# Region attention on one core: chosen regions as four index words instead of one packed word, and a row's values stored by two DMAs instead of four

## The reference, cut to what matters

```python
q_r = pool(q).transpose(0, 2, 3, 1).reshape(N, 49, C)
k_r = pool(k).reshape(N, C, 49)
_, idx_r = jax.lax.top_k(q_r @ k_r, 4)
key_g = jnp.take_along_axis(ks_[:, :, None], idx, axis=3)
val_g = jnp.take_along_axis(vs[:, :, None], idx, axis=3)
attn = jax.nn.softmax(einsum('bhnqd,bhnkd->bhnqk', qs * SCALE, key_g), -1)
out = einsum('bhnqk,bhnkd->bhnqd', attn, val_g)
out = out + depthwise_conv3x3(v) + lepe_b
x + (einsum('nchw,oc->nohw', out, out_w) + out_b)
```

## Time and profile before

| | |
|---|---|
| median of 3 runs | 2189.56 us (2187.88 to 2190.34) |
| the profiled execution, its own time | 2192.58 us |
| its span, first to last instruction | 2190.8 us |
| busy PE, DVE, ACT, POOL | 84%, 76%, 74%, 28% |
| granted TensorE clock, mean | 0.973 |
| DMA engines, share of their time in SP's queue | 33.0% |

### The profile page before, as it was taken

One profiled execution on the slowest core, in us unless ns is written; L12 is line 12 of the kernel. 1 busy time (PEld: TensorE's weight loads), 2 busy tenths in 40 slices (PEclk: granted clock), 3 DMA queues, 4 the chain that ended last, 5 costly groups with the idle time before them and its releaser, 6 DMA issues.

```text
span 2190.8 us, 80869 instructions
## 1 busy us (share of the span) xinstructions
PE 1837.4 (84%) x25672; PEld 1200.2 (55%) x25672; DVE 1661.0 (76%) x3843; ACT 1623.5 (74%) x5017; POOL 617.6 (28%) x1920
## 2 busy tenths in 40 slices
PE   5778888898888888898888998888888988867776
PEld 3345555565555555565556655555555555545444
DVE  4678878788887878788887888878887877766544
ACT  2448878687887787788787878777887877766664
POOL 0013323232332232333232323322323232323222
PEclk9999999999999999999999999999999999998998
DMA  3213333333333333333333333333333333322323
GB/s 108 60 58 89 99 107 99 101 99 111 101 109 95 110 99 107 101 104 101 107 100 105 97 111 101 107 94 109 99 101 92 88 92 92 95 84 83 90 81 86
DMA packets 221330, 212.07 MB, mean 97 GB/s; under 512 B 19328, under 2 KB 220656, under 8 KB 220912
## 3 DMA queue, kind: packets, MB, share of 16 engines
q1 hardware_dynamic: 220912, 206.90, 33.0%
HBM read 155.45 MB, written 51.38 MB: 94 GB/s over the span
## 4 chain that ended last, share of the span: by engine, by line
SPq 69%; issue 15%; PE 8%; DMA 4%; DVE 2%; ACT 1%; POOLq 0%; POOL 0%; DVEq 0%
SPq L242 51%; SPq L210 10%; PE chunk_bank L766 4%; SPq L232 4%; DMA v_sel<-v_dram 2%; DMA v_dram<-v_stage 1%; SPq L254 1%; DVE lepe L522 1%; PE pt_bank L843 1%; SPq L259 1%; PE o_bank L857 1%; PE chunk_bank L779 1%; PE chunk_bank L755 1%; SPq L223 1%; DMA x_in<-x_dram 1%
## 5 line engine op out<-in xcount | busy, mean ns | idle before, releaser
L433 ACT ACTIVATE probs<-s_bank,neg_max 128x256 f32<-128x256 f32 x1568 | 733.6, 476 | 200.4 <-DVE neg_max L626 196.3
L313 POOL COPY k_sel<-k_all 128x128 f32 x1568 | 427.0, 307 | 1048.7 <-PE s_bank L832 1038.4
L626 DVE TENSOR_REDUCE neg_max<-s_bank 128x2 f32<-128x512 f32 x784 | 506.3, 686 | 206.7 <-PE s_bank L832 205.2
L522 DVE SCALAR_TENSOR_TENSOR lepe<-v_band,taps,lepe 128x448 f32<-128x448 f32 x896 | 612.6, 700 | 23.0 <-POOL v_band L329 13.7
L440 ACT COPY probs_t<-pt_bank 128x512 f32<-128x512 f32 x784 | 464.4, 592 | 196.7 <-PE pt_bank L843 193.5
L766 PE MATMUL chunk_bank<-xn,wqkv 128*128 128x448 f32 x1344 | 594.8, 552 | 15.0 <-ACT q_all L416 5.1
L843 PE MATMUL pt_bank<-ident,probs 128*128 128x128 f32 x3136 | 500.8, 283 | 14.3 <-ACT probs_t L440 13.0
L857 PE MATMUL o_bank<-probs_t,v_sel 128*32 128x64 f32 x12544 | 263.9, 226 | 256.9 <-DMA v_sel<-v_dram 256.0
L843 PEld LDWEIGHTS pt_bank<-ident,probs 128*128 128x128 f32 x3136 | 366.7, 143 | 157.3 <-issue 98.1
L857 PEld LDWEIGHTS o_bank<-probs_t,v_sel 128*32 128x32 f32 x12544 | 199.0, 112 | 430.8 <-DMA v_sel<-v_dram 403.1
L433 ACT ACTIVATION_READ_ACCUMULATOR probs<-s_bank,neg_max 128x1 f32 x1568 | 318.9, 203 | 0.0
(11 more groups left out here) (56 smaller groups left out, 1254.2 us busy)
## 6 DMA issues: line engine op xcount, KB each, us to landing
v_sel<-v_dram SPq DMA_DIRECT2D x1568, 64.0 KB
x_in<-x_dram SPq DMA_DIRECT2D x56, 448.0 KB, 3.9
v_dram<-v_stage SPq DMA_DIRECT2D x224, 112.0 KB
resid<-x_dram SPq DMA_DIRECT2D x56, 448.0 KB, 4.0
out_dram<-resid SPq DMA_DIRECT2D x56, 448.0 KB, 3.3
wqkv<-w_qkv_dram SPq DMA_DIRECT2D x1, 768.0 KB, 5.4
wout<-w_out_dram SPq DMA_DIRECT2D x1, 256.0 KB, 6.2
idx_row<-packed_idx SPq DMA_DIRECT2D x8, 0.2 KB
```

The costliest lines, as they stand in the source:

```text
L313: last = pool.tensor_copy(k_sel[:, r % K_SLOTS, :, RT * j:RT * (j + 1)], k_all[:, b % 2, :, bass.ds(reg[j] * RT, RT)])
L433: act.activation(probs[:, u, :], s_bank[:, u, 0:KEYS], ACT.Exp, bias=neg_max[:, r % 2, u:u + 1], accum_out=denom[:, r % 2, u:u + 1]).then_ ...
L522: ins = dve.scalar_tensor_tensor(row, v_band[:, n % BANDS, k, t // 3:t // 3 + RS, t % 3:t % 3 + W], taps[:, k, t:t + 1], row, ALU.mult, AL ...
L626: dve.tensor_reduce(neg_max[:, r % 2, 2 * hf:2 * hf + 2], s_bank[:, 2 * hf:2 * hf + 2, 0:KEYS], AX.X, ALU.max, negate=True).then_inc(max_d ...
```

## The change

What it does, part by part:

- DVE's `choose` no longer packs: three small instructions an image go, and `top_idx` (49x4 words) is what is brought into one partition, 16 bytes a region instead of 4.
- `chosen` on SP and on POOL loads four adjacent words into four registers with one load instruction. The seven shifts and masks a region go from both queues.
- A row's values are stored by two DMAs of 224 KB instead of four of 112 KB. Both halves of `v_stage` are waited for, and the two DMAs stand in slot rc=0 of the next row (in the last row of an image in rc=6, as before), with one semaphore `v_stored` for both halves. ACT's `vt_out` waits for that semaphore before it writes either half.
- `affinity` shares memory with a part of `qk_mean` that is no longer read by then.

```diff
-        def chosen(eng, r):
-            n = r % NREG
-            word = eng.value_load(idx_row[0:1, (r // NREG) % 2, n:n + 1])
-            return [nc.s_assert_within((word >> (IDX_BITS * j)) & (2 ** IDX_BITS - 1), 0, NREG - 1,
-                                       skip_runtime_bounds_check_because="max_index gives one of the 49 regions")
-                    for j in range(TOPK)]
+        def chosen(engine, r):
+            first = TOPK * (r % NREG)
+            return nc.values_load_multi_w_load_instructions(
+                idx_row[0:1, (r // NREG) % 2, first:first + TOPK], engines=[engine], min_val=0, max_val=NREG - 1,
+                skip_runtime_bounds_check_because="max_index gives one of the 49 regions")[1]
...
-            def store_values(n, m):
+            def store_values(n):
                 b, rr = divmod(n, NWIN)
-                wait_taken(sp, "vt", n, m)
-                if b >= 2 and rr == 0 and m == 1:
+                for m in range(2):
+                    wait_taken(sp, "vt", n, m)
+                if b >= 2 and rr == 0:
                     sp.wait_ge(attn_done, NREG * (b - 1))
                 for h in range(2):
-                    first = 4 * m + h
-                    sp.dma_start(v_dram[b % 2, first:first + 3:2, rr * W:(rr + 1) * W, :].rearrange("q t d -> t q d"),
-                                 v_stage[PADW * h:PADW * h + W, m, :, :]).then_inc(v_stored[m], 16)
+                    sp.dma_start(v_dram[b % 2, h:RS:2, rr * W:(rr + 1) * W, :].rearrange("q t d -> t q d"),
+                                 v_stage[PADW * h:PADW * h + W, :, :]).then_inc(v_stored, 16)
...
-                sp.dma_start(idx_row[:, b % 2, :], packed_idx[:, 0:1]).then_inc(idx_in, 16)
+                sp.dma_start(idx_row[:, b % 2, :], top_idx[:, 0:TOPK]).then_inc(idx_in, 16)
...
-                    if rc == 1 and is_row(s + A_LEAD - 1) and rr:
-                        store_values(s + A_LEAD - 1, 0)
+                    if rc == 0 and is_row(s + A_LEAD - 1) and rr:
+                        store_values(s + A_LEAD - 1)
...
-                    if rc == 6 and is_row(s + A_LEAD):
-                        store_values(s + A_LEAD, 1)
                     if rc == 6 and rr == LAST and is_row(s + A_LEAD):
                         n = s + A_LEAD
-                        store_values(n, 0)
+                        store_values(n)
                         sp.wait_ge(idx_in, 16 * (n // NWIN + 1))
-                        sp.wait_ge(v_stored[0], 32 * (n + 1))
-                        sp.wait_ge(v_stored[1], 32 * (n + 1))
+                        sp.wait_ge(v_stored, 32 * (n + 1))
...
                 if n:
-                    act.wait_ge(v_stored[m], 32 * n)
+                    act.wait_ge(v_stored, 32 * n)
...
-                dve.tensor_copy(affinity[:], side(2 * KC * NREG, NREG)[0:NREG, :]).then_inc(aff_taken, 1)
+                dve.tensor_copy(affinity, side(2 * KC * NREG, NREG)[0:NREG, :]).then_inc(aff_taken, 1)
...
-                settle(dve.max(top[:], affinity[:]))
-                settle(dve.max_index(top_idx[:], top[:], affinity[:]))
-                word = top_idx[:, TOPK - 1:TOPK]
-                for j in range(TOPK - 2, -1, -1):
-                    ins = dve.scalar_tensor_tensor(packed_idx[:, j:j + 1], word, float(2 ** IDX_BITS),
-                                                   top_idx[:, j:j + 1], ALU.mult, ALU.add)
-                    word = packed_idx[:, j:j + 1]
-                    if j:
-                        settle(ins)
-                    else:
-                        ins.then_inc(top_done, 1)
+                settle(dve.max(top[:], affinity))
+                dve.max_index(top_idx[:], top[:], affinity).then_inc(top_done, 1)
```

More of the change, by code:

```diff
@@ L7 @@
 U32 = mybir.dt.uint32
-I32 = mybir.dt.int32
 ALU = mybir.AluOpType
@@ L37 @@
 LAST_TAP = KC * (TAPS - 1) - KC
-IDX_BITS = 6
 V_SLOTS = 3
@@ L99, in attention_kernel @@
         v_band = sb("v_band", [P, BANDS, KC, RS + 2, PADW])
-        v_stage = sb("v_stage", [TWO, 2, 2, C])
+        v_stage = sb("v_stage", [TWO, 4, C])
         resid = sb("resid", [TT, 2, NT, C])
@@ L125, in attention_kernel @@
         qk_mean = sb("qk_mean", [P, 2 * KC, NREG])
-        affinity = sb("affinity", [NREG, NREG])
+        affinity = qk_mean[0:NREG, 0, :]
         top = sb("top", [NREG, 8])
         top_idx = sb("top_idx", [NREG, 8], U32)
-        packed_idx = sb("packed_idx", [NREG, TOPK], I32)
-        idx_row = sb("idx_row", [1, 2, NREG], I32)
+        idx_row = sb("idx_row", [1, 2, TOPK * NREG], U32)
         s_bank = ctx.enter_context(nc.psum_tensor("s_bank", [P, HG, 512], F32))
@@ L138, in attention_kernel @@
         x_loaded = [sem(f"x_loaded{i}") for i in range(2)]
-        v_stored = [sem(f"v_stored{i}") for i in range(2)]
+        v_stored = sem("v_stored")
         v_sel_in = [sem(f"v_sel_in{i}") for i in range(V_SLOTS)]
@@ L223, in load_x @@
                 sp.dma_start(x_in[:, n % 2, :, :], x_rows[n]).then_inc(x_loaded[n % 2], 16)
-            def store_values(n, m):
+            def store_values(n):
                 b, rr = divmod(n, NWIN)
-                wait_taken(sp, "vt", n, m)
-                if b >= 2 and rr == 0 and m == 1:
+                for m in range(2):
+                    wait_taken(sp, "vt", n, m)
+                if b >= 2 and rr == 0:
                     sp.wait_ge(attn_done, NREG * (b - 1))
                 for h in range(2):
-                    first = 4 * m + h
-                    sp.dma_start(v_dram[b % 2, first:first + 3:2, rr * W:(rr + 1) * W, :].rearrange("q t d -> t q d"),
-                                 v_stage[PADW * h:PADW * h + W, m, :, :]).then_inc(v_stored[m], 16)
+                    sp.dma_start(v_dram[b % 2, h:RS:2, rr * W:(rr + 1) * W, :].rearrange("q t d -> t q d"),
+                                 v_stage[PADW * h:PADW * h + W, :, :]).then_inc(v_stored, 16)
             def select_values(r):
-                reg = chosen(sp, r)
+                reg = chosen(mybir.EngineType.SP, r)
                 if r >= V_SLOTS:
@@ L308, in gather_keys @@
                     wait_taken(pool, "k", b * NWIN + LAST, 1)
-                reg = chosen(pool, r)
+                reg = chosen(mybir.EngineType.Pool, r)
                 if r >= K_SLOTS:
@@ L404, in vt_out @@
                 if n:
-                    act.wait_ge(v_stored[m], 32 * n)
+                    act.wait_ge(v_stored, 32 * n)
                 wait_full(act, "vt", n, m)
                 bank = bank_of("vt", n, m)
-                act.copy(v_stage[:, m, :, :].rearrange("p q c -> p (q c)"), bank[0:TWO, :]).then_inc(free("vt", n, m), 1)
+                act.copy(v_stage[:, 2 * m:2 * m + 2, :].rearrange("p q c -> p (q c)"), bank[0:TWO, :]).then_inc(free("vt", n, m), 1)
             def q_out(n, k):
```

## The result

| | before | after |
|---|---|---|
| median of 4 runs | 2188.72 us | 1961.90 us (1959.60 to 1964.08) |
| ratio | | 0.896, 95% interval 0.895 to 0.898 |
| the profiled execution, own time | 2192.58 us | 1963.54 us |
| busy PE, DVE, ACT, POOL | 84%, 76%, 74%, 28% | 92%, 83%, 81%, 31% |

What follows compares the result with a forecast made beforehand. SP's queue was taken as the bound. Against the profiled 2192.6 us, -198 -46 -2 +176 = -70 gave 2122.6, and the runs' median 3.0 lower gave 2120; range for 8 in 10 was 2005 to 2215.

Steps and rivals of the forecast that it cites:

- What bounds: Whole kernel: SP's queue is saturated from the first region to the last, at 5.07 us a region; PE's 84% is not the limit.
- Shifts and masks, -198: SP's queue: seven register instructions a region go, 0.50 us each region, 198 us over 392 regions.
- Stores, -46: SP's queue: one store pair a row goes at 0.94 us, 49 rows under attention, 46 us.
- new wait: SP's wait for both v_stage halves, ACT's for all of v_stored: costed at nothing; rival of ACT stopping, 2169, chance 0.02.
- An image's end, -2: Stores before the index load: two issues instead of four save 3 us, some 1 us is lost before attention.
- The load of four words, +176: SP's register load: three more words at 0.15 us each, 0.45 us a region, 176 us over 392 regions.
- signs of being wrong: Load median outside 0.93 to 1.23, DMA issues changing their 0.62, or PE's v_sel wait falling without a shorter SP row.
- The rival of one trip: SP's load: all four words come in one trip, 4.65 us a region, 2019 us; chance 0.30 with cases to 0.10 a word.
- new line of SP's waits: In the one-trip case SP's queue would get a line waiting for PE's attention.
- The range's lower end: Forecast range for 8 in 10: 2005 us, the one-trip case with a chain of 4.6 us a region.

Runs made afterwards that it cites:

- single loads: Changed kernel with four load instructions of one word each instead of one of four: 2383.03 us, ratio 1.090.
- shifted words: Changed kernel with index words shifted two places, each group of four starting 8 bytes behind a multiple of 16: 2261.15 us, ratio 1.034.
- four-word load alone: Kernel before with only the four-word load, its four stores a row kept: 1993.51 us, ratio 0.912.
- two-stores run: Kernel before with only the two stores a row, packed words and register instructions kept: 2155.49 us, ratio 0.985.
- two-region kernel: Changed kernel with SP loading the eight words of two regions in one instruction at every second region, POOL as before: 1902.06 us, ratio 0.869.

## Why the prediction was wrong, point by point

**What bounds: right.** SP's queue, from the first region to the last. The kernel follows the length of that queue in both directions: 193 and 31 us less for the parts, 421 more with single loads, 299 more with the shifted words, and no change when PE gets less work.

**Shifts and masks, -198: right in size.** The part alone gives 193 with 12 us of words inside, so about 205. The extra is about what the pauses of 0.37 us in the queue gave back, which I had counted at nothing. In the traces they come after every 128 instructions of SP's queue: 65 of them in the kernel before, 24.0 us in sum, and 44 with the four-word load alone, 16.1 us. With a third fewer instructions there are a third fewer pauses, worth 8 us.

**Stores, -46: a third too large.** They give 31. The issue with 224 KB costs what the smaller did (0.88 for a pair, 0.90 in the earlier trace rows), as forecast. Missed was what the stores did for the load behind them: one load a row now stands behind a selection's DMA, 0.79 for 0.63, and the load behind the larger pair costs nearly as much as that, 0.76 in the middle in the two-stores run. There SP's loads take 12.5 us more in sum and its wait for the stores at the images' ends 6.0 more, so 46 becomes some 28. The changed kernel's load of four words behind the larger pair, where the earlier trace rows has 0.63:

```profile
1003.66 0.41 SPq L228
1004.08 0.04 issue
1004.12 0.84 SPq L207
```

Neither new wait bites in this kernel: no line of the profile has ACT or SP waiting for them under attention. In the two-region kernel SP does wait for `v_stage`, but at the ends of images, where the kernel before asks for both halves too.

**An image's end, -2: nothing visible.** The last store is 5.10 us on its way in place of 4.67 in the earlier trace rows, after two issues in place of four; SP's wait there rose from 24.6 to 33.4 in sum, and what the two issues saved is spent there.

**The load of four words, +176: the step that failed.** "I take 0.15 a word ... because a load has little to do but the trip, and words fetched one by one would each pay it." They were not fetched one by one. Three more words cost 0.031 us in sum, +12. That the kernel is faster, as forecast, would have come out at any price below 0.209 a word and says nothing for 0.15. With the measured term the sum gives 2120 - 164 = 1956, for 1962 measured. The bound from POOL's row, at most 0.233 a word, nearly held for a word fetched by itself: 0.220 each in the shifted group, 0.238 for the fifth word. What was wrong was to choose between "one trip" and "word by word" by plausibility as though one must hold for the chip, when where the words lie decides it. No row of the kernel before could show that, so the answer was two cases of like weight; the forecast lay between them, at a price that no load has. The signs of being wrong that it gave itself show it: the load's median is 0.812, outside 0.93 to 1.23, a row takes 31.48 in place of 34.2, and PE's wait for `v_sel` is 46.4 in place of some 190.

On the skill's figure of about 200 ns a register (Trainium skill, Runtime: NRT & Kernel Launch, "Instruction fetch mechanics"): that figure is for words in HBM, these lie in SBUF. The runs come near it for a word outside an aligned group, at 0.220 to 0.238, and lie far below it inside a group, at 0.010 a word.

**The rival of one trip was the true mechanism, and its time, 2019, was 57 too slow.** It let ACT's work and its wait for maxima stop the kernel at 4.54 a region, and raised that to 4.65 without a row. The changed kernel's row runs at 4.50 with SP still the bound, and the two-region kernel at 4.41 image starts included. SP's gain came nearly whole, since the next bound, near 4.41 a region, lies below SP's 4.50. The new line of SP's waits that the rival announced did not come either. What that next bound is was read and not shown: by the two-region kernel's chain and its 298 of 300 us it is PE, and PE's 260.35 of 300 us in the earlier trace rows already were 4.40 a region; the run that took work from PE there soon met SP again.

**The range's lower end** rested on the same chain, at 4.6 a region. It is also 3 us off its own sum: less the 3.0 between the profiled execution and the runs' median it is 2002. The measured time lies outside either.

## What to carry to other kernels

When one queue bounds, price every instruction on it with the gap behind it, and price a load of registers by what stands ahead of it, too. Keep index words in groups of four that start at a multiple of 16 bytes and load whole groups: here that decided between 1962 and 2261 us with the same instructions, where 8 bytes past such a multiple was the only other start tried. For a cost that no row shows and that has two mechanisms, give the two results; a value between them is the one that cannot come out.

## What the runs showed of the hardware that was not expected

- A register load of words in SBUF on POOL: one word 0.288, four aligned 0.318, five from an aligned start 0.556, eight 0.565, four at 8 bytes past alignment 0.947.
- On SP a load of one word right behind another load takes 0.27; after a wait 0.43; behind an x or resid load 0.46; behind a pair of 112 KB stores 0.63; behind a selection's DMA 0.79 (medians by place). The price behind DMA issues is not that of the words.
- SP's queue pauses for 0.36 to 0.37 us after every 128 instructions: 65 times in the kernel before, 43 in the changed kernel. What the pause is for, no run shows.
- SP's loads of many trips suffer behind stores. Shifted words take 2.03 us in the middle behind a pair of stores of values and 2.15 behind a store of output rows, but 1.39 behind a selection's DMA and 1.06 behind an x load. Eight words take up to 1.967 behind the stores of values, shifted words up to 2.497. The cause stays open.
